# Capping the second group's distances on POOL instead of DVE in a deformable-convolution, attention and expert kernel

## What is computed

```
x = x + deform_conv(group_norm(x))        # 3x3 taps, offsets from a 3x3 convolution
t = tokens(x)                             # 256 tokens of 32 channels per image
t = t + attention(layer_norm(t))          # 4 layers of 8 heads, linear attention
t = t + experts(layer_norm(t))            # 16 experts, each picks 8 tokens
out = images(t)

deform_conv:  y = row + ky + dy,  x = col + kx + dx,  bilinear sample of 4 corners,
              a corner outside the image counts as zero; then sum over taps and channels
```

## Time and profile before

| | us |
|---|---|
| median of 3 runs | 84.89 (84.48 to 85.83) |
| the profiled execution, its own time | 85.09 |
| its span, from the first to the last instruction | 83.2 |
| around the span | 1.9 |
| busy: PE, DVE, ACT, POOL | 73.1, 44.2, 38.5, 1.7 |
| DVE one capping instruction (128x720), one product (128x576) | 0.53, 0.75 |

### The profile page before, as it was taken

How to read it: one execution, slowest core, us unless ns; L and a number is a source line. 1 busy time by engine, 2 the same in 40 slices (tenths; PEclk the granted TensorE clock), 3 DMA queues, 4 the chain that set the end, 5 groups by cost and what they waited for, 6 DMA issues and landing times.

```text
span 83.2 us, 2329 instructions
## 1 busy us (share of the span) xinstructions
PE 73.1 (88%) x976; PEld 58.6 (70%) x976; DVE 44.2 (53%) x136; ACT 38.5 (46%) x100; POOL 1.7 (2%) x9
## 2 busy tenths in 40 slices
PE   4989999899599939988999999999989997999920
PEld 4859989887478727867567887887866576777800
DVE  0088459994999954294148233332566252733220
ACT  4212359199987832892335334253235066262110
POOL 7000000000000000000000000000000000000000
PEclk9999999999999999999999999999999999999999
DMA  0899998100000000000000000000000000000031
GB/s 16 285 251 431 423 436 318 38 0 0 0 8 4 8 0 0 0 12 0 8 0 0 0 0 8 0 0 0 0 0 8 0 0 0 0 0 0 0 96 46
DMA packets 2032, 4.98 MB, mean 60 GB/s; under 512 B 452, under 2 KB 1252, under 8 KB 1892
## 3 DMA queue, kind: packets, MB, share of 16 engines
q1 hardware_dynamic: 1732, 4.36, 14.5%
q10 hardware_dynamic: 288, 0.46, 1.5%
HBM read 4.56 MB, written 0.26 MB: 58 GB/s over the span
## 4 chain that ended last, share of the span: by engine, by line
PE 65%; ACT 14%; DVE 8%; DMA 4%; issue 4%
PE bank L760 7%; PE bank L916 6%; PE bank L794 6%; PE bank L906 6%; PE bank L816 5%; PE bank L747 4%; ACT wts L587 4%; DMA x_in<-in_x 4%; PE bank L836 4%; PE bank L944 3%; ACT hat L568 3%; PE bank L924 3%; PE bank L885 2%; ACT gn_t L579 2%; PE bank L952 2%
## 5 line engine op out<-in xcount | busy, mean ns | idle before, releaser
L323 DVE TENSOR_TENSOR hats<-hat 128x576 f32<-128x576 f32 x16 | 11.4, 750 | 0.1
L794 PE MATMUL bank<-table,hats 128*128 128x128 f32 x72 | 9.6, 279 | 1.1 <-ACT gn_t L579 1.1
L587 ACT COPY wts<-bank 128x384 f32<-128x384 f32 x24 | 10.0, 492 | 0.2
L794 PEld LDWEIGHTS bank<-table,hats 128*128 128x128 f32 x72 | 7.7, 141 | 2.3 <-issue 1.3
L760 PE MATMUL bank<-gn_pad,w_off 128*72 128x128 f32 x72 | 8.6, 273 | 0.3 <-DVE gn_pad L276 0.3
L760 PEld LDWEIGHTS bank<-gn_pad,w_off 128*72 128x72 f32 x72 | 7.9, 144 | 0.7 <-DVE gn_pad L276 0.7
L816 PE MATMUL bank<-wts,gn_t 64*32 64x96 f32 x384 | 7.2, 246 | 0.1
L593 ACT COPY samp<-bank 96x384 f32<-96x384 f32 x8 | 3.9, 482 | 6.0 <-PE bank L816 6.0
L816 PEld LDWEIGHTS bank<-wts,gn_t 64*32 64x32 f32 x384 | 5.5, 106 | 1.5 <-issue 1.2
L742 PE MATMUL bank<-warm 128*128 128x256 f32 x14 | 4.9, 523 | 1.1 <-POOL warm L232 1.1
L906 PE MATMUL bank<-q_t,gram 128*128 128x256 f32 x16 | 5.3, 412 | 0.5 <-DVE gram L420 0.4
(11 more groups left out here) (118 smaller groups left out, 115.3 us busy)
## 6 DMA issues: line engine op xcount, KB each, us to landing
v_d<-in_v_d SPq DMA_DIRECT2D x1, 2048.0 KB, 10.1
q_t<-in_q_t SPq DMA_DIRECT2D x1, 512.0 KB, 5.6
w<-in_w SPq DMA_DIRECT2D x2, 256.0 KB, 8.6
table<-in_table SPq DMA_DIRECT2D x1, 436.5 KB, 5.0
w_off<-in_w_off ACTq DMA_DIRECT2D x1, 324.0 KB
x_in<-in_x SPq DMA_DIRECT2D x2, 128.0 KB, 3.6
table<-in_table SPq DMA_DIRECT2D x1, 172.0 KB, 3.8
gate_w<-in_gate_w SPq DMA_DIRECT2D x1, 128.0 KB, 9.4
```

Source lines behind the costliest of these rows:

```text
L323: dve.tensor_tensor(hats[:, n % HB, :, h * WP:(h + 1) * WP].rearrange("p k (r q) -> p k r q", r=WR), v[:, :, 0:WR].unsqueeze(3).broadcast_ ...
L587: act.copy(wts[:, n % 2, i * KS * P:(i + 1) * KS * P], ring[i][:, 0:KS * P]).then_inc(s["evac"], 1)
L794: mm = pe.transpose(ring[ky][:, kx * P:(kx + 1) * P], hats[:, n % HB, ky * KS + kx, :], ident)
```

## The change

The two instructions of `hat_values(1, h)` leave DVE. POOL makes the same values in place, behind its five fills, each as soon as ACT's absolute value of that half is there, and counts up a semaphore of its own, `pool_hat`. Products of the second group (images 4 to 7) wait for `pool_hat` instead of `hat`.

```diff
@@ block.gpsimd
             pool.memset(hid_d[:], 0.0).then_inc(s["hid_set"], 1)
+            for h in range(HALVES):
+                pool.wait_ge(s["abs"], HALVES + h + 1)
+                pool.tensor_scalar(hat[1][:, h], hat[1][:, h], 1.0, 1.0, ALU.min,
+                                   ALU.subtract).then_inc(s["pool_hat"], 1)
@@ block.vector, hat_values(g, h)
-                i = g * HALVES + h
-                dve.wait_ge(s["abs"], i + 1)
+                dve.wait_ge(s["abs"], h + 1)
@@ block.vector, product(n, h)
-                dve.wait_ge(s["hat"], g * HALVES + h + 1)
+                dve.wait_ge(s["hat"] if g == 0 else s["pool_hat"], h + 1)
@@ block.vector, order
             distance(1, 1, off_ps[HALVES + 1][:, 0:GB * OC])
-            for h in range(HALVES):
-                hat_values(1, h)
             for h in range(HALVES):
                 product(3, h)
```

More of the change, by code:

```diff
@@ L180, in build @@
             "warm_set", "hid_set", "eps_set", "pad_set", "gn_var", "gn_std", "pad_done", "flat_done", "off_mm", "off_copy", "off_tr",
-            "off_done", "dist", "abs", "hat", "near_max", "near_n", "near_mm", "near_done", "prod", "ring_mm", "evac",
+            "off_done", "dist", "abs", "hat", "pool_hat", "near_max", "near_n", "near_mm", "near_done", "prod", "ring_mm", "evac",
             "smp_mm", "smp0_done", "smp1_done", "co_mm", "x1_done",
```

## The result

The change makes the kernel slower by a little: 85.53 us against 85.02 (medians of 21 runs each, taken side by side), a ratio of 1.0072 with a 95% interval of 1.0046 to 1.0097, or 0.4 to 0.8 us. The ratio is taken without the executions that lay over 1.5% above their kernel's fastest. The forecast was a gain of 0.96 us, with a range that ended at 85.2 us.

The account below looks back on a forecast made before the run. DVE's queue was taken to bound the stage before `contract(0)`. Image 4's products starting at 22.05 instead of 23.01 gain 0.96 us: 84.89 - 0.96 = 83.9 us; range 83.5 less 0.2 for scatter, to 85.2.

Parts of the forecast that it names:

- What bounds the kernel: In the changed stage, DVE's in-order queue up to its fourth copy of samples, including 1.05 us of idle time.
- the unnamed hole before `contract(0)`: PE's 1.37 us "issue" gap without a named releaser, claimed to be a wait for DVE's fourth copy of samples.
- I take c = 0.90 us: Assumed price of each POOL capping of 720 elements, hand-over included, with ACT's absolute value as nearest row.
- The upper end: Dearest price given for POOL's capping, reading costing as much again as a fill: 1.42 us.
- rival 3: POOL's capping costs three fills, 2.13 us, by turns, both ahead of image 3's products; 86.75 us, chance 0.10.
- POOL and DVE taking turns for whole instructions: POOL's cappings and DVE's two-SBUF-input products exclude each other; gain 0.96 us with this, 1.38 without.
- The wait: DVE waits for POOL's second capping before image 4's products, which start at 22.05 against 23.01.
- PE's floor and `decide` as caps of 1.38 us: Before `contract(0)`: PE's readiness caps the gain at 1.49 us, the chain from `decide` at 1.38.
- t = 20.25 + 2c: Start of image 4's products on DVE by turns, from POOL's price per instruction; 22.05 us forecast.
- Rival 1: POOL and DVE run side by side; with a POOL price up to 1.4, gain 1.38, 83.5 us; chance 0.30.
- the range's upper end of 85.2: Slow limit of the forecast time in us, from the case of turns with POOL at 1.1 to 1.6.

Follow-up runs that it names:

- pool_beside: Kernel before plus two POOL cappings on a spare buffer nobody reads, with DVE's real cappings in their old place; ratio 1.0027 to the kernel before.
- the probe: Kernel before plus single POOL instructions on a spare buffer late in the attention part, one after another; two-operation capping of 720 elements 2.61 us.
- pool_first_half: The change for half 0 only: POOL caps that half, DVE caps half 1 behind image 3's products; ratio 0.988 to the kernel before.
- order_pool_beside: Kernel before with DVE's second-group cappings moved behind image 3's products, plus two POOL cappings on a spare buffer; ratio 1.0064 to the kernel before.
- pool_copy: The change with POOL's capping replaced by a plain copy in place, so the output isn't the reference's; ratio 0.986 to the kernel before.
- pool_min_only: The change with POOL's minus one left out, min alone, so the output isn't the reference's; ratio 0.993 to the kernel before.
- pool_by_image: The change with POOL's two instructions cut into eight, one image and half each, in order of need; ratio 0.984 to the kernel before, median 83.45 us.

## Why the prediction was wrong

- **What bounds the kernel: right.** DVE's queue ends the unnamed hole before `contract(0)`, and what the contraction gains or loses the rest of the span keeps: ACT's last copy starts 49.17 us behind it in before and in the change, 49.18 in pool_by_image.
- **The step that failed: "I take c = 0.90 us".** POOL's capping costs 2.61 us. The upper end that I gave, twice a fill (1.42), and even rival 3's three fills (2.13) lay below. I had priced POOL by bytes, a fill and a fill again for the reading; the probe shows that reading costs 0.08 us and each arithmetic operation 0.6 to 1.2. ACT's row of the same shape (0.83 us) misled me: it says nothing of POOL's pace. The estimates that I had worked out from the Trainium skill (GPSIMD Engine Reference, sections 4.1 and 3.1), 0.60 and 1.58 us, were too low as well; the probe's copy, 0.78, is 0.18 above the first, and the capping, with 2.61, is far above both.
- **POOL and DVE taking turns for whole instructions: wrong.** With c = 2.61 rival 3's sum (18.80 + 2c + 1.34 + 0.47, both of POOL's ahead of image 3's products) would have been 25.83, a loss of 2.8 us; the loss was 0.47. Image 3's products ran inside POOL's first instruction. Contact there is, but of another form (last section).
- **The wait: the right mechanism, on the wrong instruction.** The sum looked at the first product of image 4. The one that counts is the second, behind both of POOL's instructions, in a row: 18.80 + 2 x 2.61 + 0.10 = 24.12 against 23.68, 0.44 late, measured 0.47. The same line gives the point at which the change turns from gain to loss: c = (23.68 - 18.90) / 2 = 2.39 us.
- **The gain that was there.** PE's floor and `decide` as caps of 1.38 us: measured 1.39 with a POOL instruction of 0.79 us. By the forecast's turns, t = 20.25 + 2c, that price would have given 1.18, so the mechanism would have been off even with the right price. Rival 1, side by side, described what happened better than the forecast; only its condition, c up to 1.4, did not hold, and it reckoned POOL's second result from the second absolute value instead of from the end of the first instruction.
- **The chances.** The time stayed within 2%, as forecast, but moved the other way, to 85.53; the range's upper end of 85.2 left no room for c over 1.6 other than by rival 3's large loss.

## What to carry to other kernels

Price an instruction moved to POOL by a POOL row with the same number of arithmetic operations, not by its fills or copies; here two operations on 720 elements cost 2.6 us against 0.53 on DVE. Where DVE stands idle between two instructions, first try to put ready work into the gap: that needed no other engine and gave 1.5% here, and no kernel with POOL was faster than that beyond the intervals. If slow work does go to POOL, cut it and order it by who needs it first; a consumer then waits for a piece, not for the whole.

## What the runs showed of the hardware

**A product that meets the start of POOL's instruction is held until 0.65 us of it are over.** A product of DVE reads two inputs from SBUF and takes 0.75 us. Take the end of a stretched one, less 0.75, less POOL's start:

| kernel | product | POOL's start and length | held until, behind POOL's start |
|---|---|---|---|
| the change | 20.03, 1.07 | 19.70, 2.61 | 0.65 |
| the change | 22.42, 1.26 | 22.28, 2.61 | 0.65 |
| pool_first_half | 19.02, 1.07 | 18.70, 2.61 | 0.64 |
| order_pool_beside | 20.07, 1.15 | 19.82, 2.61 | 0.65 |
| pool_copy | 19.60, 1.05 | 19.25, 0.79 | 0.65 |
| pool_min_only | 22.14, 0.92 | 21.66, 2.01 | 0.65 |
| pool_by_image (180 elements) | 25.62, 0.83 | 25.49, 0.83 | 0.21 |

It is the same for a copy of 0.79 us and a capping of 2.61, both of 720 elements, and shorter for 180 elements. That fits a time in which POOL fetches its input; that it is the fetching was not tried. The next product, inside the same POOL instruction, is not held (the change, single row):

```profile
21.02 0.74 DVE L326 TENSOR_TENSOR hats<-hat 128x576 f32<-128x576 f32 x1
```

The Trainium skill (SBUF — State Buffer, section Who interferes with whom) says that such a product contends with a GpSimd instruction that reads SBUF, and that one of the two blocks for a whole instruction. These rows agree with the contact and disagree with its length.

**The one that comes second gives way.** In pool_beside POOL's second instruction starts at 21.95, when a product (21.93 to 22.68) is under way, and takes 3.20 us, 0.59 more than by itself. A product that starts at 23.07, 1.12 us into that instruction, is held as well (0.87 us), until 1.24 behind POOL's start: the same 0.65, shifted by POOL's own 0.59. In order_pool_beside POOL's second instruction starts at 22.40 under a capping that ends at 22.82, and takes 2.88 us. Both orders of starting occur, and in these rows the later instruction pays.

**DVE's own cappings are held at the start and once more near the end of POOL's instruction.** One takes 0.53 us by itself. The one at 19.23 in pool_beside (0.94 us) is held until 0.64 behind POOL's start, like a product. But those that start 1.99 us into an instruction of 2.61 (1.01 us, in pool_first_half and order_pool_beside) are held until 2.46 and 2.47, where products run freely (a pair from 24.24 in order_pool_beside takes 1.43 us). The one that starts 1.81 us in, in pool_beside, keeps its 0.54 us, and POOL's instruction takes 2.99 instead. Why there is a second such stretch was not tried; that POOL writes its output there is a guess.

**The start scatters.** The 14 warming matmuls took 4.89 us before and 6.29 after at a granted clock of 1.00 in both. In the other ten profiled executions they took 4.67 to 6.33, and in all twelve the mark lies between 18.11 and 19.19 us. The times of the kernel before spread over 84.1 to 86.3 us; how much of that is the start was not looked into, nor its cause. It is a reason to go by distances from a mark, in which smaller differences can be seen than in the times.
